# Reordering the second layer's experts in a four-layer cross-attention kernel: shared experts first, router picks between them

## The chip, the cores and the metric

The kernel runs on one core of a Trainium2 chip as a single program. The metric is the device time of that program in microseconds (us), as the median of several runs. The core has four engines that compute and that are ordered among each other only by semaphores: TensorE (PE, matrix products), VectorE (DVE, elementwise work and reductions), ScalarE (ACT, activation functions) and GpSimd (POOL, elementwise work). SyncE (SP) issues the transfers.

## The reference, cut to what matters

Four layers, each a cross-attention and a feed-forward, run over `x` (8 x 56 = 448 tokens of width 128). The change is in the feed-forward of layer 1, counted from 0. It is a mixture of 16 routed experts, of which each token takes the two with the highest logits, weighted by a sigmoid, and of a shared expert of width 256 that every token takes with weight one:

```
logits = jnp.einsum('btc,ec->bte', x, router_w)
top_vals, top_idx = jax.lax.top_k(logits, TOP_K)          # TOP_K = 2
gates = jax.nn.sigmoid(top_vals)
w_full = zeros((N, E)).at[arange(N)[:, None], sel].add(gw)
h = jax.nn.silu(gate) * up                                # all 16 experts, all tokens
out_all = jnp.einsum('neh,ehc->nec', h, down_w)
moe = jnp.einsum('ne,nec->nc', w_full, out_all)
shared = silu(x @ shared_gate_w.T) * (x @ shared_up_w.T) @ shared_down_w.T
return moe + shared
```

The result times `tanh(g_ffn[1])` is added to `x`. The order of the sum over experts doesn't matter but for rounding.

## The kernel before, in words

The kernel computes all 16 routed experts for all tokens, and cuts the shared expert into two of width 128. So there are 18 equal experts (`E1 = 18`), each with a weight per token: the tile `wts` holds 18 columns for each of 4 groups of 112 tokens. Columns 0 to 15 are the picks times the sigmoid of the logits, columns 16 and 17 are one. The experts' matrices lie in DRAM in the order of their use, three to a load (`load_experts1`, L581, G1 = 3), in two buffers.

For expert e these steps are taken, each released by a semaphore:

- PE, `gate_up1` (L1037): two products of 128x448 for gate and up, recorded as four matmuls (L1042), into two of four banks of PSUM.
- ACT, `silu1` (L1466): silu of the gate (L1468).
- DVE, `hidden1` (L2171): silu times up, into one of two tiles; recorded at L1740, as every two-operand operation of DVE is, since the helper `tt` issues it.
- PE, the second half of `expert1` (L1046): four products by the down matrix, eight matmuls (L1055), into bank 6 or 7. It waits for `hidden1(e)` and for `weigh(e - 2)`, which empties the bank.
- DVE, `weigh` (L2175): the product out of PSUM times the expert's weight, into one of two halves of `big` (L1740, 112x512).
- POOL, `add_expert` (L1669): adds that half to the accumulator `y2` (L1671). For the first expert it waits for `weigh(0)` alone.

On PE, `expert1(e)` first issues `gate_up1(e + 1)` and then the down product of e, so PE's stream is gate-up 0, gate-up 1, down 0, gate-up 2, down 1, gate-up 3, down 2, and so on. The order of each engine's work is written by hand; nothing is planned by a program. DVE takes its instructions strictly in the order of the text.

`pick(v, n, k, low)` (L2149) finds the k-th pick of each token: seven small operations, each waiting for the one before: a maximum (L2154), a comparison, a product with a constant row of ranks, a maximum (L2157), a comparison, and then either the masking of the pick (L2160, k = 0) or the sum of both picks (k = 1). Between the picks and the loop stand three pieces of DVE work: a product of two columns (128x1) and the scaling of `w_kT2` by it (L2199), which a later layer needs; the product of picks and sigmoid into `wts`; and the memset of the two shared columns (L2202). `Chain.link` issues an operation and waits for its end before the next; `Chain.step` issues it without the wait. The loop of the other experts begins at L2207.

ACT does silu 0, silu 1, the sigmoid of the logits (L1473) and then the other silus. Silu and sigmoid need different function tables, so an ACT_TABLE_LOAD stands ahead of each switch.

Of the kernel before, what the change touches and what calls it, by code (L numbers as in the profile page):

```python
# [11 lines left out]
ALU = mybir.AluOpType  # L12
# [3 lines left out]
D = 128  # L16
# [14 lines left out]
E1 = 18  # L31
# [84 lines left out]
G1 = 3  # L116
# [76 lines left out]
def build(nc, io, out):  # L193
    ctx = ExitStack()
    with ctx:
# [54 lines left out]
        def cs(name, rows=D):  # L250
            a, b = CST[name]
            return cst[0:rows, a:b]
# [11 lines left out]
        def carve(shape, dt=F32):  # L264
            n = int(np.prod(shape[1:]))
            words = n if dt == F32 else (n + 1) // 2
            a = arena[0:shape[0], at[0]:at[0] + words]
            at[0] += words
            assert at[0] <= ARENA, at[0]
            if dt != F32:  # L270
                a = a.bitcast(dt)
            if len(shape) == 2:
                return a
            names = "abcd"[:len(shape) - 1]
            return a.rearrange("p (" + " ".join(names) + ") -> p " + " ".join(names),
                               **dict(zip(names[1:], shape[2:])))
# [74 lines left out]
        sm16 = carve([TT, 8, NT, 16])  # L351
        wts = carve([TT, NT, E1])
# [1381 lines left out]
        def _(dve):  # L1734
            ch = Chain(dve, dve_s)
# [3 lines left out]
            def tt(out, a, b, op):  # L1739
                return dve.tensor_tensor(out, a, b, op)  # L1740

            def over(col, shape):

                return col.unsqueeze(2).broadcast_to(shape)
# [404 lines left out]
            def pick(v, n, k, low):  # L2149


                rank = cs("rank", TT)[:, 0:n].unsqueeze(1).broadcast_to([TT, NT, n])
                src = v[:, k]
                ch.link(dve.tensor_reduce(acol[:, 0, :], src, AX.X, ALU.max))  # L2154
                ch.link(tt(v[:, 2], src, over(acol[:, 0, :], [TT, NT, n]), ALU.is_equal))
                ch.link(tt(v[:, 2], v[:, 2], rank, ALU.mult))
                ch.link(dve.tensor_reduce(acol[:, 1, :], v[:, 2], AX.X, ALU.max))  # L2157
                ch.link(tt(v[:, 3 + k], v[:, 2], over(acol[:, 1, :], [TT, NT, n]), ALU.is_equal))
                if k == 0:
                    ch.link(dve.scalar_tensor_tensor(v[:, 1], v[:, 3], low, src, ALU.mult, ALU.add))  # L2160
                else:
                    ch.link(tt(v[:, 5], v[:, 3], v[:, 4], ALU.add))
# [8 lines left out]
            def hidden1(e, p):  # L2171
                dve.wait_ge(ex_act, e + 1)
                tt((xT2, xT3)[p], ps[0:D, 3 + 2 * p, 0:N], exs[p], ALU.mult).then_inc(ex_h, 1)

            def weigh(e, p, weight, first):  # L2175

                dve.wait_ge(ex_dn, first + e + 1)
                dve.wait_ge(ex_acc, first + e + 1)
                tt(big[:, :, D * p:D * p + D], ps[0:TT, 6 + p, :].rearrange("p (t n) -> p t n", t=NT),
                   weight.broadcast_to([TT, NT, D]), ALU.mult).then_inc(ex_w, 1)  # L2180

            def weigh_last(k, e, weight, first):
# [5 lines left out]
                residual(k, big[:, :, D:2 * D])  # L2188
                dve.nop().then_inc(ex_acc, 1)

            hidden1(0, 0)
            dve.wait_ge(to_act, 1)
            pick(sm16, 16, 0, NEG)
            hidden1(1, 1)
            pick(sm16, 16, 1, NEG)

            dve.wait_ge(ld_m, 5 * 16)
            ch.link(tt(qk_col[:, 0:1], qk_col[:, 0:1], qk_col[:, 1:2], ALU.mult))
            ch.step(dve.tensor_scalar(w_kT2, w_kT2, qk_col[:, 0:1], 8.0, ALU.mult, ALU.mult))  # L2199
            act_in.next()  # L2200
            ch.step(tt(wts[:, :, 0:16], sm16[:, 5], sm16[:, 6], ALU.mult))
            ch.link(dve.memset(wts[:, :, 16:E1], 1.0))  # L2202

            weigh(0, 0, wts[:, :, 0:1], 0)
            hidden1(2, 0)
            weigh(1, 1, wts[:, :, 1:2], 0)
            with dve.Fori(1, E1 // 2 - 1) as i:  # L2207
                for p in range(2):
                    e = 2 * i + p
# [278 lines left out]
```

## Time and profile before

| | us |
|---|---|
| median of 3 runs | 856.37 (855.80 to 856.83) |
| the profiled execution, whole | 857.73 |
| its span (first to last instruction) | 855.9 |
| the experts of layer 1, from the first gate-up matmul to the last down matmul | 330.8 to 375.5 |
| PE busy | 754.6 (88%) |
| DVE busy | 609.3 (71%) |
| ACT busy | 418.5 (49%) |
| POOL busy | 329.4 (38%) |

Times in the rows are microseconds from the span's start. The busy shares are means over many stages with different limits, so the stage of the change has to be read by itself. A row of a timeline gives the start, the duration, the engine, the line of the code, the operation, output and inputs with their shapes, and in brackets how long the engine had been idle and what released it. Consecutive instructions of one kind are merged into one row with a count. DVE is pipelined: an instruction that waits for nothing starts before the recorded end of the one ahead.

### The profile page before, as it was taken

To read this page: it belongs to the slowest core of one execution; us is meant where nothing else is said; L and a number is where in the kernel's file an instruction comes from. 1 tells how busy PE (TensorE), PEld (TensorE's weight loads), DVE (VectorE), ACT (ScalarE), POOL (GpSimd) and SP (SyncE) were. 2 spreads that over 40 slices of the span, in tenths; PEclk is the share of its full clock that TensorE was granted. 3 is DMA by queue.
4 is the path that set the end of the run, shared out by engine and by line. 5 is a ranking of instruction groups with operands and counts; after the bars stand their busy time and mean duration, and the time that the engine had idled before them with its cause. 6 is when DMAs were issued, how large, how long until landed. Compare 5 with 4: busy or idle time off the path is not lost.

```text
span 855.9 us, 15688 instructions
## 1 busy us (share of the span) xinstructions
PE 754.6 (88%) x5632; PEld 496.1 (58%) x5632; DVE 609.3 (71%) x1264; ACT 418.5 (49%) x682; POOL 329.4 (38%) x255
## 2 busy tenths in 40 slices
PE   4599999996777979987899999997898998988997
PEld 3577777786445576653455555563246665654675
DVE  4789999998886665566555666568788997515653
ACT  2476666673465624424444545411047776734331
POOL 0665555553523602550677777721160100000111
PEclk9799999997888958999999999998869999899999
DMA  7256766432425530205023332026834767000220
GB/s 202 81 196 215 245 207 201 160 121 83 60 84 180 160 99 8 85 30 161 1 75 89 118 92 75 0 34 100 115 97 101 121 145 148 3 2 25 92 93 23
DMA packets 50583, 88.35 MB, mean 103 GB/s; under 512 B 17375, under 2 KB 34975, under 8 KB 50167
## 3 DMA queue, kind: packets, MB, share of 16 engines
q1 hardware_dynamic: 50518, 87.49, 38.1%
q8 instruction: 41, 0.67, 0.3%
q14 instruction: 24, 0.19, 0.1%
HBM read 61.97 MB, written 25.51 MB: 102 GB/s over the span
## 4 chain that ended last, share of the span: by engine, by line
PE 46%; DVE 37%; ACT 5%; issue 5%; POOL 4%; DMA 2%; SPq 0%; DVEq 0%; POOLq 0%; ACTq 0%
DVE arena L2341 8%; PE ps L1109 8%; DVE arena L1740 8%; PE ps L1099 6%; DVE rn L1895 4%; PE ps L1277 3%; DVE arena L1944 3%; PE ps L1042 3%; PE ps L1214 3%; PE ps L1287 3%; DVE arena L1923 2%; PE ps L1203 2%; DVE arena L1903 2%; POOL arena L1694 2%; ACT arena L1538 2%
## 5 line engine op out<-in xcount | busy, mean ns | idle before, releaser
L2341 DVE TENSOR_REDUCE arena<-ps 112x1 f32<-112x500 f32 x192 | 114.9, 669 | 15.9 <-PE ps L1186 15.8
L1740 DVE TENSOR_TENSOR arena<-ps,arena 128x448 f32<-128x448 f32 (+7 forms) x138 | 83.4, 629 | 58.4 <-ACT arena L1562 19.7
L1694 POOL TENSOR_TENSOR arena<-arena 125x448 f32<-125x448 f32 x96 | 109.5, 1141 | 24.2 <-ACT arena L1507 21.2
L1109 PE MATMUL ps<-arena 125*128 125x448 f32 (+1 forms) x208 | 97.1, 548 | 1.4 <-ACT arena L1507 0.9
L1538 ACT ACTIVATE arena<-ps 125x896 f32<-125x896 f32 x96 | 87.0, 917 | 21.8 <-PE ps L1203 21.6
L1507 ACT ACTIVATE arena<-arena,kbias 125x448 f32<-125x448 f32 x96 | 63.7, 668 | 65.3 <-DVE arena L1740 46.3
L1740 DVE TENSOR_TENSOR arena<-ps,rn 125x448 f32<-125x448 f32 x96 | 59.3, 618 | 47.7 <-PE ps L1099 43.3
L1099 PE MATMUL ps<-arena 128*125 128x448 f16 (+3 forms) x312 | 77.9, 360 | 3.0 <-DVEq L1751 3.0
L1099 PEld LDWEIGHTS ps<-arena 128*125 128x125 f16 (+1 forms) x312 | 40.9, 135 | 57.2 <-issue 42.3
L801 PE MATMUL ps<-w_k2h,arena 128*125 128x512 f16 x288 | 67.9, 388 | 6.8 <-ACT arena L1343 5.2
L1671 POOL TENSOR_TENSOR arena<-arena 112x512 f32<-112x512 f32 x24 | 30.4, 1267 | 89.5 <-DVE arena L1740 89.4
L1343 ACT ACTIVATE arena<-ps 125x512 f32<-125x512 f32 x96 | 55.8, 596 | 14.2 <-PE ps L801 11.1
L1214 PE MATMUL ps<-arena 125*32 125x168 f32 x768 | 49.9, 331 | 11.5 <-ACT arena L1538 8.7
L1895 DVE TENSOR_REDUCE rn<-arena 125x8 f32<-125x512 f32 x96 | 58.2, 677 | 0.0
L1186 PE MATMUL ps<-arena 64*112 64x500 f16 x192 | 54.8, 443 | 2.9 <-DVE arena L2341 1.5
L801 PEld LDWEIGHTS ps<-w_k2h,arena 128*125 128x125 f16 x288 | 39.2, 139 | 30.4 <-ACT arena L1343 8.3
L1589 POOL TENSOR_TENSOR arena<-arena 112x4 f32<-112x4 f32 x9 | 9.3, 1028 | 121.5 <-DVE arena L1764 113.7
L824 PE MATMUL ps<-w_l,arena 128*125 128x256 f32 x192 | 44.7, 390 | 4.3 <-ACT arena L1370 4.3
L1712 POOL COPY arena<-arena 125x1152 f32<-125x1152 f32 x8 | 9.2, 1147 | 97.0 <-PE ps L1218 84.8
L1109 PEld LDWEIGHTS ps<-arena 125*128 125x128 f32 (+1 forms) x208 | 37.8, 189 | 13.9 <-issue 8.4
L728 PE MATMUL ps<-w_k2h 128*128 128x512 f16 x192 | 45.6, 393 | 0.0
L1605 POOL TENSOR_TENSOR arena<-arena 128x500 f16<-128x500 f32 x24 | 29.2, 1218 | 40.8 <-ACT arena L1330 40.8
(305 smaller groups left out, 1496.1 us busy)
## 6 DMA issues: line engine op xcount, KB each, us to landing
arena<-in_ctxT SPq DMA_DIRECT2D x8, 750.0 KB, 8.1
d_cln<-arena SPq DMA_DIRECT2D x8, 750.0 KB
d_clnT<-arena SPq DMA_DIRECT2D x8, 750.0 KB
d_k<-arena SPq DMA_DIRECT2D x24, 250.0 KB
d_v<-arena SPq DMA_DIRECT2D x24, 250.0 KB
arena<-d_clnT SPq DMA_DIRECT2D x8, 750.0 KB
arena<-in_ctx SPq DMA_DIRECT2D x8, 672.0 KB
arena<-d_cln SPq DMA_DIRECT2D x8, 672.0 KB
```

Of the source, the lines that this page charges most:

```text
L801: mm = pe.matmul(ps[0:KP, k, :], clnT[p][:, a, KP * j:KP * j + KP], w_k2h[:, w, :], start=(n == 0), stop=(n == 2))
L1099: mm = pe.matmul(ps[0:rows, (t + p) % 2, 0:N].rearrange("p (h q) -> p h q", h=H8), clnT_s[p][:, a, cols:cols + rows], qtT[:, q, :, bass.ds ...
L1109: pe.matmul(ps[0:D, 4 + 2 * p, 0:N], cln_s[p][0:rows, t, :], pexp[(t + p) % 2][0:rows], start=(t == 0), stop=(t == KT)).then_inc(l2_pv, 1)
L1186: pe.matmul(ps[0:TT, max_bank(bn, u), 0:500], q.rearrange("p o h q -> p (o h q)"), kst[bn % 3][64 * r:64 * r + 64, g, 500 * third:500 * th ...
L1214: pe.matmul(ps[32 * g:32 * g + 32, 6, 0:168], v3s[p][:, t, 32 * g:32 * g + 32], p3[t % 2][:, 3 * g:3 * g + 3, :].rearrange("p h q -> p (h ...
L1343: act.activation(sqk[:, j % SQ, :], ps[0:KP, k, :], ACT.Square).then_inc(a_free, 1)
L1507: act.activation(pexp[(t + p) % 2][0:rows], sscl[(t + p) % 2][0:rows], ACT.Exp, bias=bias)\
L1538: act.activation(p3[t % 2].rearrange("p (k h) q -> p k (h q)", k=2), ps[0:KP, 2 * (t % 2):2 * (t % 2) + 2, 0:8 * S], ACT.Exp).then_inc(l3_ ...
L1694: ins = pool.tensor_tensor(psum2[p][0:rows], psum2[p][0:rows], pexp[(t + p) % 2][0:rows], ALU.add)
L1740: return dve.tensor_tensor(out, a, b, op)
L1895: dve.tensor_reduce(rn[:, bass.ds(turn - 1, 1), j, :].rearrange("p o h -> p (o h)"), sqk[:, j % SQ, :].rearrange("p (h d) -> p h d", h=H8) ...
L2341: dve.tensor_reduce(mx3[bn % 2][:, u % 2, u % 8 // 2, u // 8:u // 8 + 1], ps[0:TT, max_bank_of(bn, u), 0:500], AX.X, ALU.max).then_inc(l3_ ...
```

## The change

The two shared experts become experts 0 and 1, and the sixteen routed ones 2 to 17. Their columns in `wts` move along, and so do the matrices in DRAM. As their weight is one and is set ahead of everything, `weigh(0)` no longer stands behind the picks: it is issued between the two picks, and `weigh(1)` behind `hidden1(2)`. The column product, the scaling of `w_kT2` and the product into `wts` now follow `weigh(1)`, and the last of them is a `link`. The memset of the weights of one stands ahead of `hidden1(0)`. PE, ACT, POOL and SP have the same instructions as before.

```diff
+            ch.link(dve.memset(wts[:, :, 0:2], 1.0))
             hidden1(0, 0)
             dve.wait_ge(to_act, 1)
             pick(sm16, 16, 0, NEG)
             hidden1(1, 1)
+            weigh(0, 0, wts[:, :, 0:1], 0)
             pick(sm16, 16, 1, NEG)
+            hidden1(2, 0)
+            weigh(1, 1, wts[:, :, 1:2], 0)

             dve.wait_ge(ld_m, 5 * 16)
             ch.link(tt(qk_col[:, 0:1], qk_col[:, 0:1], qk_col[:, 1:2], ALU.mult))
             ch.step(dve.tensor_scalar(w_kT2, w_kT2, qk_col[:, 0:1], 8.0, ALU.mult, ALU.mult))
             act_in.next()
-            ch.step(tt(wts[:, :, 0:16], sm16[:, 5], sm16[:, 6], ALU.mult))
-            ch.link(dve.memset(wts[:, :, 16:E1], 1.0))
-
-            weigh(0, 0, wts[:, :, 0:1], 0)
-            hidden1(2, 0)
-            weigh(1, 1, wts[:, :, 1:2], 0)
+            ch.link(tt(wts[:, :, 2:E1], sm16[:, 5], sm16[:, 6], ALU.mult))
+
             with dve.Fori(1, E1 // 2 - 1) as i:
...
-        "L1_ex": np.concatenate([experts1, np.stack(shared1)]).reshape(-1, G1, D, 3 * D).transpose(0, 2, 1, 3)
+        "L1_ex": np.concatenate([np.stack(shared1), experts1]).reshape(-1, G1, D, 3 * D).transpose(0, 2, 1, 3)
```

## Rows read from the trace of the kernel before

**Rows 1.** The chain that ended last, shares of the span by engine.

```profile
PE 46%; DVE 37%; ACT 5%; issue 5%; POOL 4%; DMA 2%; SPq 0%; DVEq 0%; POOLq 0%; ACTq 0%
```

**Rows 2.** Stretches: us, busy us of PE, PEld, DVE, ACT, POOL, clock, DMA share, GB/s.

```profile
336.30:340.00 3.70, 3.08 (x18) 1.99 (x17) 3.48 (x12) 2.84 (x4) 0.97 (x1) 1.00 0.01 2
344.80:347.18 2.38, 2.38 (x14) 1.62 (x13) 1.22 (x2) 1.83 (x3) 1.26 (x2) 1.00 0.00 0
384.00:388.00 4.00, 3.93 (x6) 1.50 (x6) 1.35 (x3) 0.68 (x2) 0.52 (x1) 0.57 0.32 99
```

**Rows 3.** The waits of 330 to 376 us: in total, times, longest.

```profile
PE ps L1055 <- DVE arena L1740: 1.1, 2, 0.6
```

**Rows 4.** PE's timeline, 333.5 to 342.4 us: gate-up 3, down 2, gate-up 4, down 3.

```profile
337.16 1.67 PE L1042 MATMUL ps<-arena,wex 128*128 128x448 f32 x4
339.44 1.13 PE L1055 MATMUL ps<-wex,arena 128*112 128x128 f32 x8 [0.62 <-DVE arena L1740]
340.41 1.67 PE L1042 MATMUL ps<-arena,wex 128*128 128x448 f32 x4
341.91 0.71 PE L1055 MATMUL ps<-wex,arena 128*112 128x128 f32 x5
```

**Rows 5.** DVE's timeline in the same stretch.

```profile
335.21 0.62 DVE L1740 TENSOR_TENSOR arena<-ps,arena 128x448 f32<-128x448 f32 x1
335.76 0.21 DVE L2154 TENSOR_REDUCE arena<-arena 112x4 f32<-112x64 f32 x1
336.00 0.23 DVE L1740 TENSOR_TENSOR arena<-arena 112x64 f32<-112x64 f32 x1
336.26 0.23 DVE L1740 TENSOR_TENSOR arena<-arena,cst 112x64 f32<-112x64 f32 x1
...
338.17 0.69 DVE L1740 TENSOR_TENSOR arena<-ps,arena 112x512 f32<-112x512 f32 x1
```

**Rows 6.** The chain that ended last, 337 to 339 us: start, duration, piece.

```profile
337.29 0.17 DVE arena L1740
...
337.49 0.18 DVE arena L2199
...
337.89 0.22 DVE arena L1740
...
338.77 0.63 DVE arena L1740
```

**Rows 7.** ACT's timeline there, the third silu last.

```profile
337.49 0.54 ACT L1468 ACTIVATE arena<-ps 128x448 f32<-128x448 f32 x1
```

**Rows 8.** POOL's timeline, 326 to 342 us.

```profile
339.03 3.96 POOL L1671 TENSOR_TENSOR arena<-arena 112x512 f32<-112x512 f32 x3 [11.36 <-DVE arena L1740]
```

**Rows 9.** POOL and DVE at 797 to 801 us; that DVE form's durations, ns min/median/max.

```profile
798.18 1.27 POOL L1671 TENSOR_TENSOR arena<-arena 112x512 f32<-112x512 f32 x1 [23.30 <-DVE arena L1740]
...
798.46 2.08 DVE L1740 TENSOR_TENSOR arena<-wex,arena 128x1024 f16<-128x1024 f32 x1
...
L1740 DVE TENSOR_TENSOR arena<-wex,arena x8: 1224/1226/2078, 778.3 to 832.7; 128x1024 f16<-128x1024 f32 x8
```

**Rows 10.** The same two engines at 26 us; L1909's durations, ns min/median/max.

```profile
26.01 1.27 POOL L1597 TENSOR_TENSOR wex<-wex,vec 112x512 f32<-112x512 f32 x1
...
26.18 1.13 DVE L1909 TENSOR_SCALAR arena<-arena 125x12 f32<-125x12 f32 x1
...
L1909 DVE TENSOR_SCALAR arena<-arena x8: 173/173/1131, 15.1 to 163.0; 125x12 f32<-125x12 f32 x8
```

**Rows 11.** The same two at 416 us, and L1694's mean (ns) over the kernel.

```profile
416.42 0.47 DVE L1843 TENSOR_SCALAR arena<-arena,wscale 128x512 f32<-128x512 f32 x1
...
416.63 1.27 POOL L1694 TENSOR_TENSOR arena<-arena 125x448 f32<-125x448 f32 x1
...
L1694 POOL TENSOR_TENSOR arena<-arena 125x448 f32<-125x448 f32 x96 | 109.5, 1141 | 24.2 <-ACT arena L1507 21.2
```

**Rows 12.** The landing of the transfers into `wex`.

```profile
DMA to landing us min/median/max: 3.4/3.7/10.8
```

## The prediction

> **What bounds the kernel now.** I read the chain that ended last first. Half of it is PE, most of the rest DVE, and transfers are 2% [rows 1], so a delay inside the chain goes through to the end. Then the stage itself. In the steady part of the expert loop, one expert takes 2.38 us and PE is busy in all 2.38, with DVE at 1.22 and POOL at 1.26 [rows 2]: the loop is bound by PE, and nothing on DVE matters there while its work fits into the 1.16 us left over. The waits then say that in the whole stage PE stood for DVE twice, with 0.6 us the longest [rows 3]. PE's timeline places it: gate-up 3 starts at 337.16 and down 2 at 339.44, where the next gate-up 4 (340.41) is followed by down 3 at 341.91, 1.50 us later [rows 4]. Without the wait down 2 would start at 337.16 + 1.50 = 338.66. So 339.44 - 338.66 = 0.78 us can be had, and about 0.1 more because a down product behind a wait takes 339.44 to 340.41, 0.97 us, instead of 2.38 - 1.50 = 0.88. The change can give no more than 0.87 us, 0.10% of the kernel. What down 2 waits for is `hidden1(2)`, at 338.77 [rows 6], the last of a row of DVE instructions: `hidden1(1)` at 335.21, the second pick from 335.76 [rows 5], the column product at 337.29, the scaling at 337.49, the weights at 337.89 and `weigh(0)` at 338.17 [rows 5, 6].
>
> **The change part by part, DVE alone.** The memset goes ahead of `hidden1(0)`, where DVE waits for ACT: nothing. `hidden1(1)` stays at 335.21, as do all of ACT's steps. `weigh(0)` follows after 0.55 us (335.21 to 335.76), at 335.76; down 0 ended long before. It takes 0.69, and the next instruction starts 0.60 behind it (338.17 to 338.77) [rows 5, 6]. So the second pick moves from 335.76 to 336.36 and its end, where the column product stood, from 337.29 to 337.89. `hidden1(2)` also needs silu 2, which ends at 337.49 + 0.54 = 338.03 [rows 7]; with 0.04 for the release it could start at 338.07. That is 0.70 before its 338.77. Were this all, down 2 would be at 338.74.
>
> **What is then late.** `weigh(0)` also releases POOL. Before, POOL was idle for 11.36 us and started the first add at 339.03 [rows 8], that is 0.17 behind the end of `weigh(0)` (338.17 + 0.69), when DVE's remaining work read one operand from PSUM. Now the add starts at 335.76 + 0.69 + 0.17 = 336.62, in the middle of the second pick, whose comparisons and products have two operands in SBUF. What that costs the rows show at other places. At 798.18 the same add (1.27 us) is running when DVE comes with a two-operand instruction from SBUF at 798.46: it takes 2.08 instead of 1.23, so it began in effect at 799.31, 0.14 before the add's end [rows 9]. A tiny scaling of 125x12 behind a POOL instruction takes 1.13 instead of 0.17, again from 0.14 before POOL's end [rows 10]. The Trainium skill, SBUF — State Buffer, section "Who interferes with whom", gives it as a lock: a DVE instruction with two SBUF inputs, or in a two-port mode, and a GpSimd instruction that reads SBUF exclude each other for the whole instruction, and the one issued second waits. By that rule, too, POOL's add stops the pick, and the change that frees DVE's order has an engine beside it that takes the time back; without it the sum would be C's, below.
>
> Collision 1, in the pick. Its first comparison moves from 336.00 to 336.60, the product from 336.26 to 336.86 [rows 5]. The comparison is 0.02 ahead of the add; the product then meets it, and starts at 336.62 + 1.27 - 0.14 = 337.75 or, with the add itself held a little by the comparison, up to 337.9: 0.9 to 1.05 late. If the comparison is the one held, 337.75 - 336.60 = 1.15 late. I take 1.0. `hidden1(2)` is then at 337.89 + 1.0 = 338.89, +0.12 against before, and down 2 at 339.56.
>
> Collision 2, in the moved block. `weigh(1)` starts 0.55 behind, at 339.44, ends at 340.13 and releases the second add at 340.30. The column product stands at 339.44 + 0.60 = 340.04 and the scaling 0.20 behind it at 340.24 [rows 6], just ahead of the add. A scaling from SBUF delays a POOL instruction that starts 0.21 behind it by 0.13 (1.27 against 1.14 [rows 11]), that is until 0.34 after its own start; so the add runs from 340.58 to 341.85. The weights product, due 0.40 behind the scaling [rows 6] at 340.64, is held until 341.85 - 0.14 = 341.71 and ends at 341.93. If the add is first and the scaling is held, this is 0.1 later. Behind it stands all of DVE's queue: the loop's start, `hidden1(3)`, `weigh(2)`. The product is now waited for ahead of the loop's header. No row shows that header bare: before, it lay hidden in the 0.60 us between the starts of `weigh(0)` and `hidden1(2)` [rows 5, 6]. Between nothing and 0.60 I take 0.2, as it is a few register instructions, each shorter than the shortest row. `hidden1(3)` is at 342.13, ends 0.62 later at 342.75, and down 3 is at 342.79, where before it was at 341.91: +0.88, and with the 0.09 of a down product behind a wait, +0.97. PE itself would have been there at 339.56 + 0.97 + 1.50 = 342.03, so PE stands 0.90 ahead of down 2 and 0.76 ahead of down 3.
>
> After that `hidden1(4)` needs silu 4 (gate-up 4 ended by 342.2, silu done by 342.8) and DVE, free by 343.3; down 4 is due at 345.2. DVE has caught up, and the loop runs at 2.38 again, 0.97 late. The order of the experts changes no product: same shapes, and the same loads of three. The third load, issued behind down 2 and landing in 3.7 us [rows 12], moves by 0.1 and is needed only at gate-up 6, two periods later than down 3. SP's queue holds nothing else there. The rest of the kernel follows unchanged.
>
> The sum: the profiled execution took 857.73 whole with a span of 855.9, and would take 858.7 with 856.9. The median before is 1.36 lower than that execution; on its scale the forecast is 856.37 + 0.97 = 857.3.
>
> **The rivals.** (B) Only the first collision happens, or the weights product slips in ahead of the waiting add. Then it ends at 340.86, `hidden1(3)` by 341.8, before PE needs it, and only the +0.12 stays: 856.5. For it: the two starts differ by hundredths. Against: POOL has been waiting by then, and DVE leaves a gap. (C) The two engines don't collide, because an add whose operands are short on DVE's side lets it through: down 2 at 338.74 is 0.70 early, the block ends at 340.2, `hidden1(3)` at 341.1, just ahead of down 3's 341.21, and the gain stays whole: 855.7. For it: no row shows an operation of the pick itself beside an add. Against: rows 9 and 10, where a form of 12 elements was held like the one of 1024. (D) Slower than can be mistaken: PE's clock. It is granted 1.00, its upper level of 2.4 GHz, in the stretches of the stage shown [rows 2]. Two waits of 0.90 and 0.76 us within 4 us make PE less busy than anywhere in the expert stage so far. If the clock falls to 1.2 GHz behind them as it does at 384 to 388, where 4 us are granted 0.57 [rows 2], a PE that is the bound loses 0.43 x 4 = 1.7 us: 857.3 + 1.7 = 859.0. It decides from the two waits together; against it, that the stretch with the wait of 0.62, 336.3 to 340, is granted 1.00 [rows 2].
>
> **How the numbers follow.** A change of 0.2%, 1.7 us, is about what a measurement here can tell from none. Forecast 0.53, B 0.14, C 0.20, D 0.10, anything else 0.03. The forecast's own range is 856.5 to 858.4: 0.2 less or 0.4 more for the header, 0.15 either way for the first collision, and 0.5 for the medians, which spread over 855.80 to 856.83. C with that spread sets the low end at 855.2, D the high end at 858.9. Faster by 0.2% (below 854.66) is only C with luck in the clock of later stages: 0.04. Slower (above 858.08): nearly all of D and a seventh of the forecast, 0.17. The same: 0.79.
>
> **What would show it.** Right: the first add of POOL starts near 336.6; one small operation of the second pick takes over 1 us instead of 0.23; the weights product takes over 1 us; PE shows two waits, ahead of down 2 and of down 3, of 0.7 to 1.0 us. Wrong: if the small operations keep their 0.23 beside the add (C), if PE's second wait is missing (B), or if the granted clock is below 1.00 between 340 and 376 (D). If the stage from the first gate-up to the last down product isn't about 1 us longer, the prediction's mechanism has failed, wherever the median lies.

## The result, and the profile after

The changed kernel took 868.22 us in the median of 4 runs (865.38 to 869.9), the kernel before 856.09 (4 runs, 855.4 to 856.83): a ratio of 1.0121, 95% interval 1.009 to 1.0152. Every ratio in this document leaves out runs more than 1.5% above the fastest of their kernel; none of these eight is such a run. The forecast was 857.3, the range 855.2 to 858.9. It was wrong by 11 us. The profiled execution after took 868.92 whole, with a span of 867.1 against 855.9.

The stage that the prediction worked out did what it said. DVE's timeline of the kernel after (start, duration, line, operation; "x2" joins two neighbours):

```profile
334.22 1.22 DVE L1740 TENSOR_TENSOR arena<-ps,arena 128x448 f32<-128x448 f32 x2
335.36 0.21 DVE L2154 TENSOR_REDUCE arena<-arena 112x4 f32<-112x64 f32 x1
335.60 0.23 DVE L1740 TENSOR_TENSOR arena<-arena 112x64 f32<-112x64 f32 x1
335.86 1.17 DVE L1740 TENSOR_TENSOR arena<-arena,cst 112x64 f32<-112x64 f32 x1
337.06 0.22 DVE L2157 TENSOR_REDUCE arena<-arena 112x4 f32<-112x64 f32 x1
...
337.84 1.22 DVE L1740 TENSOR_TENSOR arena<-ps,arena 128x448 f32<-128x448 f32 x2
338.98 0.15 DVE L1740 TENSOR_TENSOR arena<-arena 128x1 f32<-128x1 f32 x1
339.16 1.60 DVE L2203 TENSOR_SCALAR arena<-arena 128x512 f32<-128x512 f32 x1
340.68 0.21 DVE L1740 TENSOR_TENSOR arena<-arena 112x64 f32<-112x64 f32 x1
341.12 0.62 DVE L1740 TENSOR_TENSOR arena<-ps,arena 128x448 f32<-128x448 f32 x1 [0.23 <-DVE arena L1740]
```

POOL's timeline of the same kernel, and then PE's:

```profile
335.61 1.33 POOL L1671 TENSOR_TENSOR arena<-arena 112x512 f32<-112x512 f32 x1 [8.96 <-DVE arena L1740]
339.20 1.27 POOL L1671 TENSOR_TENSOR arena<-arena 112x512 f32<-112x512 f32 x1 [2.26 <-DVE arena L1740]
```

```profile
338.52 1.13 PE L1055 MATMUL ps<-wex,arena 128*112 128x128 f32 x8 [0.69 <-DVE arena L1740]
339.48 1.67 PE L1042 MATMUL ps<-arena,wex 128*128 128x448 f32 x4
341.80 1.13 PE L1055 MATMUL ps<-wex,arena 128*112 128x128 f32 x8 [0.65 <-DVE arena L1740]
```

All this is about a microsecond earlier than in the trace before, because this execution came to the stage earlier; count from `hidden1(1)`, at 335.21 before [rows 5] and at 334.22 now. Collision 1 is there: the add starts at 335.61, and the pick's product takes 1.17 where it took 0.23 [rows 5]. Collision 2 is there too, with the scaling as its victim: 1.60 beside the add of 339.20. PE's timeline has two waits where it had one [rows 4], 0.69 and 0.65; the other wait of rows 3, of 0.51, lies ahead of the last down product (at 374.39 before), far behind the change. Down 2 comes 4.30 behind `hidden1(1)` (before 4.23), down 3 comes 7.58 behind (before 6.70): +0.88.

Now the whole kernel in stretches, the view that the prediction did not take. The borders are the first gate-up of layer 1's experts, their last down product, the first product at L1099, the first at L1145, and the start and end of layer 3's attention. First before, then after (columns: from and to, us, busy us of PE, PEld, DVE, ACT, POOL with their counts, granted clock, DMA share, GB/s):

```profile
330.77:375.49 44.72, 43.59 (x219) 29.29 (x219) 24.91 (x52) 21.59 (x28) 20.77 (x17) 1.00 0.16 53
375.49:408.56 33.07, 23.71 (x81) 10.74 (x79) 22.14 (x42) 11.52 (x20) 4.85 (x3) 0.94 0.41 112
408.56:561.61 153.05, 151.45 (x537) 81.76 (x537) 90.26 (x143) 75.48 (x109) 116.92 (x104) 0.99 0.22 63
561.61:609.34 47.73, 39.92 (x225) 22.14 (x224) 35.44 (x100) 2.53 (x5) 7.50 (x9) 0.93 0.55 81
609.34:758.37 149.03, 134.52 (x2504) 85.38 (x2504) 115.87 (x202) 99.69 (x121) 24.30 (x23) 0.90 0.50 98
```

```profile
329.71:375.47 45.76, 43.91 (x219) 29.20 (x219) 26.85 (x52) 21.59 (x28) 20.85 (x17) 1.00 0.16 52
375.47:410.03 34.56, 25.20 (x82) 12.24 (x80) 22.13 (x42) 11.52 (x20) 4.85 (x3) 0.90 0.41 107
410.03:564.29 154.26, 152.83 (x537) 82.27 (x537) 91.56 (x143) 75.50 (x109) 116.62 (x104) 0.98 0.21 63
564.29:611.93 47.64, 39.94 (x226) 21.99 (x225) 35.44 (x100) 2.54 (x5) 7.50 (x9) 0.93 0.55 86
611.93:769.06 157.13, 143.03 (x2504) 89.40 (x2504) 116.28 (x202) 100.59 (x121) 24.30 (x23) 0.84 0.44 92
```

Read the first row of each, and then the last. The stage is 45.76 - 44.72 = 1.04 longer, the forecast's +0.97. The code of every later stretch is the same in both kernels, POOL works as long as before, DVE too but for 1.30 us in the third row, and yet these stretches are 1.49, 1.21, -0.09 and 8.10 longer. In the stretches that grew, PE is busy for longer with as many instructions, and its granted clock is lower: 0.94 to 0.90, 0.99 to 0.98, 0.90 to 0.84. Outside these rows the start is 1.06 shorter and the tail 0.54 longer; all together that is the 11.2 between the spans.

Layer 3's attention runs in batches. In both kernels PE waits at L1214 once in each, and in five of them the wait is 0.89 us. Two of these waits on PE's timeline, before and then after:

```profile
646.80 0.49 PE L1214 MATMUL ps<-arena 125*32 125x168 f32 x8 [0.89 <-ACT arena L1538]
647.11 0.28 PE L1218 MATMUL ps<-arena 125*16 125x56 f32 x8
```

```profile
649.35 0.67 PE L1214 MATMUL ps<-arena 125*32 125x168 f32 x8 [0.89 <-ACT arena L1538]
649.77 0.43 PE L1218 MATMUL ps<-arena 125*16 125x56 f32 x8
```

The wait is the same, and what follows is not: right behind it the same eight matmuls take 0.67 instead of 0.49, as PE has fallen from its 2.4 GHz to 1.2 GHz. The stretches between such waits, before and then after:

```profile
646.80:662.62 15.82, 14.67 (x313) 10.02 (x313) 14.41 (x26) 12.12 (x16) 1.59 (x2) 1.00 0.60 124
662.62:678.45 15.83, 14.67 (x314) 10.02 (x314) 14.42 (x26) 12.13 (x16) 1.60 (x2) 1.00 0.71 124
```

```profile
649.35:666.59 17.24, 16.09 (x313) 10.67 (x313) 14.50 (x26) 12.28 (x16) 1.59 (x2) 0.90 0.55 113
666.59:683.81 17.22, 16.06 (x313) 10.69 (x314) 14.51 (x26) 12.29 (x16) 1.60 (x2) 0.90 0.58 115
```

A batch of 15.82 us at full clock becomes one of 17.24 with a part at half clock, PE 1.42 us longer busy, and the period longer by as much. DVE, busy for 14.4 of the 15.82, did not make up for it. The page shows it as a longer wait of DVE's reductions for PE, 22.7 us in all where it was 15.9:

```profile
L2341 DVE TENSOR_REDUCE arena<-ps 112x1 f32<-112x500 f32 x192 | 115.3, 668 | 22.7 <-PE ps L1186 22.7
```

So the open question was why a stage that is 1 us longer changes the clock in a stretch that starts 236 us after it. Two theories stood at the start, content and arrival; the third came when the kernel before turned out to spread. **Content**: the changed order itself, or the collisions, do something that lasts. **Arrival**: only when the later stretches begin decides, whatever delayed them. **Constant**: the change costs 12 us in every execution, against which stood that the time of one kernel may vary from execution to execution.

### The profile page after: what moved, and what is told of

Its sections match the earlier page's. It is cut to its first block, busy times and chain, and to the rows that moved or that the text cites. A ratio compares the mean times of both kernels' runs of the same rounds, so it can differ in the third digit from the quotient of the medians.

```text
span 867.1 us, 15689 instructions
## 1 busy us (share of the span) xinstructions
PE 765.8 (88%) x5632; PEld 502.0 (58%) x5632; DVE 614.2 (71%) x1264; ACT 419.6 (48%) x682; POOL 329.4 (38%) x255
## 4 chain that ended last, share of the span: by engine, by line
PE 46%; DVE 37%; issue 5%; ACT 5%; POOL 5%; DMA 2%; SPq 0%; DVEq 0%; POOLq 0%; ACTq 0%
PE ps L1109 8%; DVE arena L1740 8%; DVE arena L2341 7%; PE ps L1099 6%; DVE rn L1895 4%; PE ps L1214 3%; PE ps L1277 3%; DVE arena L1944 3%; PE ps L1287 2%; PE ps L1042 2%; PE ps L1203 2%; DVE arena L1923 2%; DVE arena L1903 2%; POOL arena L1694 2%; PE ps L1186 1%
## 5 line engine op out<-in xcount | busy, mean ns | idle before, releaser
L2341 DVE TENSOR_REDUCE arena<-ps 112x1 f32<-112x500 f32 x192 | 115.3, 668 | 22.7 <-PE ps L1186 22.7
L1694 POOL TENSOR_TENSOR arena<-arena 125x448 f32<-125x448 f32 x96 | 109.2, 1137 | 26.2 <-ACT arena L1507 23.3
L1099 PE MATMUL ps<-arena 128*125 128x448 f16 (+3 forms) x312 | 78.1, 360 | 3.0 <-DVEq L1751 3.0
L1099 PEld LDWEIGHTS ps<-arena 128*125 128x125 f16 (+1 forms) x312 | 40.9, 135 | 57.8 <-issue 42.4
L801 PE MATMUL ps<-w_k2h,arena 128*125 128x512 f16 x288 | 66.0, 380 | 7.2 <-ACT arena L1343 5.6
L1214 PE MATMUL ps<-arena 125*32 125x168 f32 x768 | 53.2, 350 | 11.2 <-ACT arena L1538 7.9
L1186 PE MATMUL ps<-arena 64*112 64x500 f16 x192 | 56.6, 462 | 2.8 <-DVE arena L2341 1.3
L1895 DVE TENSOR_REDUCE rn<-arena 125x8 f32<-125x512 f32 x96 | 58.2, 674 | 0.0
L1203 PE MATMUL ps<-arena 64*125 64x112 f16 x768 | 46.6, 247 | 0.0
```

Source lines behind the costliest of these rows:

```text
L801: mm = pe.matmul(ps[0:KP, k, :], clnT[p][:, a, KP * j:KP * j + KP], w_k2h[:, w, :], start=(n == 0), stop=(n == 2))
L1099: mm = pe.matmul(ps[0:rows, (t + p) % 2, 0:N].rearrange("p (h q) -> p h q", h=H8), clnT_s[p][:, a, cols:cols + rows], qtT[:, q, :, bass.ds ...
L1186: pe.matmul(ps[0:TT, max_bank(bn, u), 0:500], q.rearrange("p o h q -> p (o h q)"), kst[bn % 3][64 * r:64 * r + 64, g, 500 * third:500 * th ...
L1203: mm = pe.matmul(ps[0:KP, 2 * (t % 2) + r, 112 * g:112 * g + 112], kst[b % 3][rows, g, KP * t:KP * t + KP], qst3[rows, b:b + 1, g, 2 * r:2 ...
L1214: pe.matmul(ps[32 * g:32 * g + 32, 6, 0:168], v3s[p][:, t, 32 * g:32 * g + 32], p3[t % 2][:, 3 * g:3 * g + 3, :].rearrange("p h q -> p (h ...
L1694: ins = pool.tensor_tensor(psum2[p][0:rows], psum2[p][0:rows], pexp[(t + p) % 2][0:rows], ALU.add)
```

## The experiments

Edits are against the kernel before unless it says "after". Each result is the median over all executions with the range and their count, beside the kernel before on the same chip at the same time. Since here the spread is itself the effect, I give the difference of the means over all runs as well, with its 95% interval. The lengths of stretches are worked out from the records of each trace, as in the two tables above: E the expert stage, P the preparation behind it, A2 and A3 the attention of layers 2 and 3, counted from 0. Behind a length stands, in brackets, how much of it was granted the lower clock:

```
                  E             P             A2            A3           span
before       44.72 (0)     33.07 (3.7)   153.05 (3.2)  149.03 (30.7)  855.9
after        45.76 (0)     34.56 (6.8)   154.26 (6.8)  157.13 (51.2)  867.1
e5  = after  45.77 (0)     34.57 (6.8)   154.28 (6.8)  153.15 (44.4)  861.7
e15 = after  45.76 (0)     31.38 (0)     153.03 (3.4)  149.71 (30.7)  855.9
e1           45.73 (0)     34.58 (6.8)   154.26 (6.8)  156.14 (47.8)  866.0
e9           45.22 (0)     35.28 (10.2)  152.68 (3.4)  152.71 (44.4)  860.4
e10          48.43 (3.4)   34.57 (6.8)   154.27 (6.8)  157.27 (51.2)  867.5
e2           44.35 (0)     33.08 (3.5)   153.04 (3.3)  149.70 (30.7)  856.9
e3           44.19 (0)     33.63 (7.2)   153.04 (3.1)  149.28 (30.7)  855.3
e4           44.80 (0)     33.09 (3.8)   153.05 (3.1)  149.47 (30.7)  854.2
e11          44.09 (0)     33.61 (7.0)   153.04 (3.2)  149.19 (30.7)  854.5
e16 = e11    44.09 (0)     33.62 (7.0)   153.04 (3.2)  149.32 (30.7)  855.5
e6           44.71 (0)     33.07 (3.7)   153.04 (3.2)  149.13 (30.7)  855.8
e12          44.71 (0)     33.60 (7.6)   155.55 (9.5)  149.90 (30.7)  859.8
e13          44.72 (0)     33.08 (3.6)   153.04 (3.2)  154.73 (47.8)  859.5
e14          44.71 (0)     35.29 (10.2)  152.92 (3.4)  154.81 (47.8)  859.8
```

### A bare delay in the kernel before

```diff
 weigh(0, ...)
+for _ in range(4):
+    ch.link(dve.tensor_reduce(acol[:, 1, :], sm16[:, 2], AX.X, ALU.max))
 hidden1(2, 0)
```

> The kernel before with four small reductions (112x64 to 112x4, each waited for, some 0.245 us each) put ahead of hidden1(2): nothing of the change, only its delay of 1.0 us at the same place. Theory clock (the stage itself is 1.0 us longer, the other 11 us are PE's clock at its lower level in later stages, set by how late the work of those stages arrives): 867 to 869 us, with the stage 1.0 longer and the same stretches at half clock as in the changed kernel. Theory content (the rest comes from something else that the change brings, such as the new order of weights or POOL's earlier adds): 857.1.

It took 865.33 (855.77 to 869.65, n 10) against 860.46 (852.32 to 867.53, n 31): ratio 1.0014 [0.9965, 1.0063], difference of the means +3.8 ± 3.4. The median lies 2 below the 867 to 869 that were expected. The trace is the clear part. With the order, the adds and the scaling of before, and 1.01 us of delay, the trace has the stretches of after nearly to the hundredth (34.58, 154.26, 156.14). Its last stretch:

```profile
612.04:768.18 156.14, 141.50 (x2503) 88.48 (x2504) 116.33 (x202) 100.40 (x121) 24.33 (x23) 0.85 0.44 92
```

Content falls: neither the new order nor a collision is needed. The median of before beside this run, 860.46 and not 856, was the first sign that 4 executions were too few.

The same with 2 and with 8 reductions, to see whether the loss grows with the delay or has a threshold:

> The kernel before with two reductions (0.5 us in all) ahead of hidden1(2), half of the delay of the run with four. The four profiles of kernels with a stage 1.0 us longer all show half-clock stretches near 393, 400 and 410 to 417 where the others show one at 384 and one at 408, and need 3.7 us more from the down products to 415 us. Theory threshold (which stretches are granted turns over at some arrival between 0.15 and 1.0 us late): the profile shows one pattern or the other whole, so +0.5 or about +3.2 to 3.7 at 415 us, nothing between. Theory proportional: about +1.9.

> The same with eight reductions, 2.0 us. Theory threshold: the stretches follow the arrival in bands, so twice the delay need not cost more than the 1.0 us did: between +2 and +5 at 415 us. Theory proportional: about +7.4.

e9 took 861.52 (858.06 to 867.67, n 10) against 858.12 (853.9 to 868.63, n 35), 1.0034 [1.0005, 1.0064], means +2.6 ± 2.2; e10 took 863.52 (860.13 to 869.24, n 10), 1.0044 [1.0012, 1.0075], +4.9 ± 2.2. A stage that is 0.50 longer has 3.7 more in A3; one that is 3.71 longer has 8.2 in A3, as after has. The loss is not in proportion to the delay. Neither theory's numbers came, though: from the first gate-up to the end of A2, e9 is 2.3 longer and e10 6.4, where threshold wanted 0.5 or 3.2 to 3.7 and 2 to 5, and proportional 1.9 and 7.4; e9 shows a third pattern of falls, with 10.2 us in P. e10 also shows rival D's mechanism, at a larger wait than the change makes. PE's timeline of e10:

```profile
337.29 1.13 PE L1055 MATMUL ps<-wex,arena 128*112 128x128 f32 x8 [2.65 <-DVE arena L1740]
338.25 2.87 PE L1042 MATMUL ps<-arena,wex 128*128 128x448 f32 x4
340.92 1.57 PE L1055 MATMUL ps<-wex,arena 128*112 128x128 f32 x8
```

Behind a wait of 2.65 us the gate-up takes 2.87 instead of 1.67: 3.4 us at half clock. This is why 2 us of delay made the stage 3.71 longer.

### The two collisions

Hold POOL's adds back (on after), or scale `w_kT2` ahead of `hidden1(0, 0)` (on before, on after), or both (on after):

```diff
 # e2, e11, e16: POOL's loop of the adds
+if e == 0:
+    pool.wait_ge(ex_h, 5)
 pool.wait_ge(ex_acc, e + 2)
 # e3, e4, e11, e16: the three lines moved up
+dve.wait_ge(ld_m, 5 * 16)
+ch.link(tt(qk_col[:, 0:1], qk_col[:, 0:1], qk_col[:, 1:2], ALU.mult))
+ch.step(dve.tensor_scalar(w_kT2, w_kT2, qk_col[:, 0:1], 8.0, ...))
 hidden1(0, 0)
```

> The changed kernel, but POOL's first add also waits for hidden1(3), so that it runs beside no operation of the pick and of the moved block. If the collisions with POOL are what makes the stage 1.0 us longer, the stage gets 0.7 us shorter than before the change and no small DVE operation takes over 0.3 us. Theory clock: the whole then follows from where -0.7 us puts the later stages, which nobody can say from the rows: anything from 850 to 866, with the difference to 855.4 in the stretches at half clock. Theory content: 866.

> The kernel before with the column product and the scaling of w_kT2 moved ahead of hidden1(0), where DVE waits for ACT. down 2 waits 0.6 us less, so the stage is 0.6 us shorter; no add is near. Theory clock: 855.5 if the later stages keep their stretches at half clock, several us more or less if not. Theory content: 855.5 in any case.

> The changed kernel with the same move: the first collision (pick against add) stays, the second has nothing left but the weights product, which comes 0.2 us before the second add. The stage is 0.1 to 0.2 us longer than before the change. Theory clock: at 0.15 us the later stages lie almost as in the kernel before: 856 to 857. Theory content: 867.

> The changed kernel with both causes of its longer stage taken away: the scaling of w_kT2 ahead of hidden1(0), and POOL's first add behind hidden1(3). The stage is 0.7 to 0.8 us shorter than before the change, no DVE operation of the pick is stretched. Mean over executions 0 to 3 us below the kernel before, if the later stages keep their usual stretches; if any move of the stage were bad, above it.

> The version with the scaling early and the first add late once more. Mean 0.5 to 2 us below the kernel before; rival: no difference, or above.

The expert stage answers each edit, against 44.72 before and 45.76 after. The adds held back take 1.41 off after's stage (44.35); 0.7 less than before was expected, and it is 0.37. The scaling moved ahead takes 0.96 off after's (44.80) and 0.53 off before's (44.19). Both together give 44.09, 0.63 less than before and 1.67 less than after. But e3 has 0.53 of this without any of the reordering, so the new order adds only 0.10 to it. DVE's timeline of e11, where nothing is held and each small operation is back at 0.23:

```profile
334.98 0.23 DVE L1742 TENSOR_TENSOR arena<-arena 112x64 f32<-112x64 f32 x1
335.24 0.23 DVE L1742 TENSOR_TENSOR arena<-arena,cst 112x64 f32<-112x64 f32 x1
335.50 0.22 DVE L2159 TENSOR_REDUCE arena<-arena 112x4 f32<-112x64 f32 x1
```

Of PE's waits for DVE only the one of 0.5 us ahead of the last down product is listed; of the one ahead of down 2, 0.62 before, 0.15 is left (down 2 is 1.65 behind its gate-up, where the loop has 1.50):

```profile
PE ps L1055 <- DVE arena L1742: 0.5, 1, 0.5
```

The version that shows what the collisions cost is e2, as it differs from after in nothing but the held add. Counted from the first gate-up, its down 2 and down 3 come at 8.04 and 10.51, where before has 8.67 and 11.14 and after 8.81 and 12.10. So the mechanism is shown: the two engines' collisions turned a gain of 0.63 at these steps (the forecast for DVE alone was 0.70) into a loss. Holding the add has a price of its own, which leaves e2 with 0.37 at the stage's end. DVE then stands 1.62 us for POOL ahead of `weigh(2)`, and down 4 and the gate-up behind it come 0.17 and 0.27 later than in e11, where DVE has the scaling behind it already:

```profile
342.76 3.38 DVE L1742 TENSOR_TENSOR arena<-ps,arena 112x512 f32<-112x512 f32 x5 [1.62 <-POOL arena L1671]
```

The whole kernels do not follow. In medians, against 860.46 for e2 to e4, 858.12 (e11) and 857.75 (e16): e2 858.99 (854.3 to 866.38, n 10), ratio 0.9993 [0.995, 1.0036]; e3 858.53 (856.77 to 866.84, n 10), 0.9985 [0.9949, 1.0021]; e4 857.93 (853.16 to 866.73, n 10), 1.0005 [0.9963, 1.0047]; e11 857.01 (854.93 to 865.81, n 12), 0.9987 [0.9958, 1.0016]; e16, the same kernel, 859.49 (856.12 to 867.15, n 12), 1.0033 [1.0002, 1.0064]. By means e11 is 1.3 below before and e16 1.5 above; pooled, 24 executions against the 67 of before beside them, they are 0.1 ± 1.6 us from it. The version that was to beat both kernels beats after and equals before; a gain of 0.63 is below what this spread lets one see.

### The same kernel again: constant or not

> The changed kernel itself, beside the kernel before on one chip, with more executions of both. The kernel before has meanwhile been seen from 852 to 867 us, so four executions of each may have caught two ends. Theory mixture (a real effect of 1.0 us, the rest is which half-clock stretches an execution gets): the median lies 1 to 5 us above the median before, with the two ranges overlapping. Theory constant (the change costs 12 us in every execution): the median lies 10 to 13 us above and the ranges hardly overlap.

> The changed kernel once more. Mean 3 to 5 us above the kernel before of the same chip; the first comparison's 12 us was four draws from each end. Rival: near 12.

After unchanged, twice. e5: 863.64 (853.85 to 870.48, n 12) against 857.31 (852.09 to 869.05, n 28), 1.0037 [0.9997, 1.0076], means +4.1 ± 3.4. e15: 866.09 (853.49 to 871.05, n 12), 1.0034 [0.9989, 1.008], +5.75 ± 3.5. The profile of e15 has the same stage, 45.76, with the same two held operations, and then none of the loss. The two rows of e15 that answer to P and A3:

```profile
376.01:407.39 31.38, 22.02 (x82) 10.22 (x80) 22.14 (x42) 11.52 (x20) 4.85 (x3) 1.00 0.44 118
608.32:758.03 149.71, 134.53 (x2504) 85.46 (x2504) 115.79 (x202) 99.74 (x121) 24.33 (x23) 0.90 0.47 97
```

Its batches take 15.82 at a clock of 1.00, as those of before do. So the same code loses 8 us in A3 in one execution (the profile after), 4.1 in another (e5) and 0.7 in a third. Constant falls. Over all runs behind the first comparison the kernel before has 126 executions between 852.09 and 869.05 (mean 859.2, median 858.2), and after has 24 between 853.49 and 871.05 (mean 863.7, median 865.1). 14% of the first lie above 864, and 14 of the 24. Against the 60 executions of before beside them (mean 858.8), the means differ by 5.0 ± 2.4 us, 0.6%. That is the best estimate of what the change costs; the first comparison, with four executions of before that all fell at 855.4 to 856.83, put it at 12.

### A delay far from the experts

The arrival theory has a sharper test: leave the experts of layer 1 alone and come a little later to layer 3. e6 adds one small reduction on DVE ahead of `maxima(b)`, inside the attention. e13 and e14 add one and two ahead of the scaling of layer 3's queries, which everything behind waits for:

```diff
+ch.link(dve.tensor_reduce(acol[:, 1, :], lnst, AX.X, ALU.max))   # e14: twice
 ch.link(dve.tensor_scalar(xT2, ps[0:D, 1, 0:N], float(D) ** -0.5, ...
```

> The kernel before with one reduction (112x24 to 112x4, some 0.2 us with its wait) put on DVE ahead of the first maximum of layer 3's attention; the experts of layer 1 are untouched. Theory arrival (whether PE's clock falls once in each batch of layer 3's attention depends on tenths of a microsecond in the arrival of that stage): the profiled execution shows stretches at half clock between 645 and 760 us as the changed kernel's did, and takes 864 to 867. Theory amount (it takes the whole microsecond, or something in the experts stage): the profile of the stage stays as before, 856.6.

> The kernel before with one reduction (112x24 to 112x4, some 0.2 us with its wait) on DVE's chain of products that make layer 3's queries, near 600 us; the experts of layer 1 untouched. Theory arrival: all profiles in which the work of this stage comes 0.15 to 0.3 us later show half-clock stretches once in a batch and 152 to 157 us for layer 3's attention, the others none and 149; so here the attention takes 152 to 157. Rival (the stretches need the whole late state from 390 us on): 149.1.

> The same with two reductions, 0.4 us. Theory arrival: the bad band begins between 0 and 0.2 us and was seen up to 1.4 us later in the run with a delay of 0.5 us, so 152 to 157 for the attention here too. Rival: 149.1.

e6 took 859.29 (855.11 to 862.51, n 12), 1.0018 [0.9993, 1.0043]. A3 stayed at 149.13: the delay was hidden behind a wait for PE, so it tested nothing and is inconclusive. e13 took 861.61 (853.58 to 865.91, n 10) against 857.75 (852.38 to 866.19, n 32), 1.0031 [0.9995, 1.0067], means +2.4 ± 2.4. e14 took 861.76 (859.6 to 866.1, n 7), 1.0056 [1.0021, 1.0091], +4.2 ± 2.0. In e13's trace everything up to layer 3 is as before (44.72, 33.08, 153.04), the stretch with the added reduction is 0.23 longer, and then:

```profile
607.78:762.51 154.73, 141.97 (x2504) 88.75 (x2504) 116.25 (x202) 100.65 (x121) 24.33 (x23) 0.85 0.44 93
645.19:661.95 16.76, 16.03 (x313) 10.59 (x313) 14.07 (x25) 11.86 (x15) 1.59 (x2) 0.90 0.53 116
```

Against 609.34:758.37, an instruction of 0.2 us is followed by 5.70 more in the attention, with the clock at 0.85 instead of 0.90 and PE busy 7.45 longer. This is one profile each, of kernels whose executions spread, and the means of e13 hardly leave zero. e14 shows why a single profile can mislead: its P is 35.29 with 10.2 us at half clock, though its edit lies 230 us behind P, so that execution was in a late state by itself.

What supports arrival more is in the traces together: they record when the granted clock changes, and arrival has to be counted from there, not from the span's start. Take PE's last rise to the upper clock ahead of A3 (589.21 in before, the end of the fall near 582). A3's first product comes 19.92 to 20.19 us behind it in the nine traces whose batches have no fall (before 20.14, e15 19.98, the latest e3 and e4 with 20.19), and 20.28 to 20.43 in six of the seven whose batches have (after 20.43, e1 20.38, e13 20.32, e14 20.28); the seventh, e9, whose fall near 585 lasted 3.4 us and not 6.8 as in the others, has 22.38. From the span's start the two groups are mixed: e13 falls with 607.77, e12 does not with 611.86. P is ordered alike, by the end of the expert stage behind the last rise ahead of the stage (326.38 in before): 48.47 to 49.18 with 3.5 to 7.6 us at half clock, 49.63 and 49.88 with 10.2 (e9, e14), 50.06 to 50.21 with 6.8 (e1, e5, after), and 50.50 with none (e15); e10 has 53.51, with a fall inside the stage. Equal code draws its place here: the first gate-up comes 4.29, 4.44 and 4.74 behind that rise in e5, after and e15. So arrival holds: each execution draws its place against the clock's changes, the edit adds its delay to it, and 0.2 us can decide. That is a reading of sixteen traces, made behind the runs; the one edit that moves A3's arrival alone is e13, from before's 20.14 to 20.32.

### Attempts to keep the clock up

Fill PE's waits: at the first step of each batch the max product is repeated three times into its own bank (e7 on after, e8 on before), meant for the wait of 0.89 us. Or fill most of PE's wait at 381.1 to 382.9 us with more of the kernel's own keep-busy products (e12):

```diff
 # e7, e8
+for _ in range(3 if t == 0 and n else 0):
+    pe.matmul(...)                        # the same product as the next
 pe.matmul(ps[0:TT, bank, 0:500], ...)
 # e12
-keep_clock(26, 3)
+keep_clock(33, 3)
```

> The changed kernel with three extra matmuls of 64x112 by 500 in each batch of layer 3's attention but the last, repeating the one behind them in the text, ahead of the place where PE waits 0.89 us for ACT once in a batch. Theory: this wait is what the clock falls behind (at 649.35 the wait ends, at 649.5 the clock falls). Then the wait shrinks to 0.1 to 0.3, no half-clock stretch stands between 645 and 725, and the median is 7 to 9 us lower than the changed kernel's. Rival: the stretches come from elsewhere in the batch, or DVE's maxima wait for the extra matmuls: same or slower.

> The kernel before with the same three extra matmuls for each batch. Theory: its own executions above 860 us are those with the half-clock stretches in layer 3's attention, so the median falls from about 860 to 855, the range narrows to some 6 us, and the difference between this and the changed kernel with the same matmuls is 1.0 us plus what the stretches at 384 to 417 us give (up to 4). Rival: no effect on the range.

> The kernel before with 33 instead of 26 dummy matmuls behind the experts, which fill 1.5 of the 1.8 us in which PE waits at 381.1 to 382.9 for the layer norm. Theory: the clock falls at 384.4 behind that wait, and the 3.4 us at half clock there cost 1.7 us; with the gap filled there is no fall at 384 and the span is 1 to 2 us shorter, unless a fall moves to the gaps at 391 to 409 behind it. Rival: the wait has no part in the fall, same time.

e7 took 867.86 (861.91 to 869.14, n 6), ratio 1.0113 [1.0078, 1.0148], means +8.0 ± 2.7; e8 took 861.98 (856.19 to 869.3, n 11), 1.0057 [1.0024, 1.009], +3.8 ± 2.9. The products missed the wait. It is 0.89 in both kernels still; only the first one, of 1.58, shrank to 0.33. Two of e8's waits, with no fall near:

```profile
646.39 0.49 PE L1219 MATMUL ps<-arena 125*32 125x168 f32 x8 [0.89 <-ACT arena L1543]
662.79 0.49 PE L1219 MATMUL ps<-arena 125*32 125x168 f32 x8 [0.89 <-ACT arena L1543]
```

The batch between them takes 16.40 where before has 15.82, so the products lie on the path and cost 0.58 us in each at full clock. In e7 batches with a part at half clock stayed. Whether the fall comes from the 0.89 us wait is therefore not tested by either run. e12 took 861.64 (858.42 to 864.59, n 12), 1.0027 [1.0004, 1.0051], +2.5 ± 1.5: the wait shrank from 1.83 to 0.31 and the half clock at 384 went, and more of it came later, 7.6 us in P and 9.5 in A2 where there were 3.7 and 3.2. The rows of e12:

```profile
374.77:408.37 33.60, 25.76 (x89) 12.11 (x87) 22.13 (x42) 11.51 (x20) 4.84 (x3) 0.89 0.44 110
408.37:563.92 155.55, 154.12 (x537) 82.85 (x538) 91.12 (x143) 75.50 (x109) 116.74 (x104) 0.97 0.21 62
```

All three expectations of a gain were missed, and e8's range did not narrow.

## Why the prediction was wrong

- **DVE alone (-0.70): right.** In e2, where no add is near, down 2 comes 3.53 behind `hidden1(1)` (339.02 and 335.49 in its timelines), 0.70 less than the 4.23 before, and down 3 is 0.70 earlier as well. A small term was missed: from the first gate-up to `hidden1(1)` it is 4.51 in after, e2 and e15 and 4.44 before. Those 0.07, with the +0.88 of down 3 and the 0.09 of a down product behind a wait, are the 1.04. The memset alone does not make them: e4, e11 and e16 have it and show 4.44 to 4.45; what does is open. That e2 keeps only 0.37 at the stage's end is the cost of holding the add, above.
- **Collision 1: right, in place and price.** The add began 0.17 behind the end of `weigh(0)`, as forecast, the comparison kept its 0.23, the product took 1.17 against 0.23: 0.94 late (forecast 1.0). Down 2 stands +0.07 against `hidden1(1)` (forecast +0.12). The Trainium skill, SBUF — State Buffer, section "Who interferes with whom", says that the one that comes second is blocked for the whole instruction, not slowed, and that a reduction never is; the trace agrees. The 64-element product takes 1.17. The pick's own reduction, at 337.06, came behind the add's end and shows nothing, but in the trace of before 87 reductions at L1895 (125x512) lie beside a POOL instruction and take 0.67 to 0.68 us, as the nine others do.
- **Collision 2: right in sum, wrong in its victim.** The scaling was to be just ahead of the add and the weights product held. In the trace the scaling's record starts 0.04 before the add's and it is the one held, 1.60 against 0.49; the product then took its 0.21. The prediction had this as its alternative, "0.1 later", and the loop's header cost 0.23 (forecast 0.2). Down 3: +0.88, as forecast, with some luck: down 2 came 0.05 less late than forecast, and the way from there to down 3 was 0.05 longer. The stage: +1.04 against +0.97.
- **Rivals B and C: out**, by PE's second wait and by the held operations. One sum of C was off: its own steps from 338.07 end at 340.04, not 340.2; nothing hangs on it. **Rival D: out in its place.** The stage is granted 1.00 behind two waits of 0.69 and 0.65; it took one of 2.65 to bring the clock down there (e10).
- **"The rest of the kernel follows unchanged": this is the step that failed.** It was true of the instructions and false of their durations. The later stretches grew by 1.49, 1.21 and 8.10 us with the clock. The warning stood in the rows: before's own 384 to 388 us is granted 0.57 [rows 2], so this kernel's clock falls behind waits that it has anyway, and I asked only whether the change makes a new wait, not whether it shifts the old ones. The traces of e1 and e13 show that shifting them by 1.0 or 0.2 us is enough, and the sixteen traces, that what decides is where the stage starts behind the clock's last rise.
- **"0.2%, about what a measurement here can tell": too small.** It rested on three executions within 1.03 us. Over 126 the same kernel spreads over 17 us (2%). The range ought to have been several times as wide upward, as before itself lies above 864 in one of seven executions.

What stays open is how a given execution will come out. The executions differ from each other already before the experts of layer 1 (the first stretch is 326.6 to 331.0 us in the sixteen traces, with 51 to 61 us at half clock), so each execution reaches the later waits at another moment, and none of this can be known ahead. Nor does a run here change the length of the 0.89 us wait. The Trainium skill, TensorE: Matmul & The Clock Gate, section "Part 1: The HAM clock gate (the "warmup" mystery)", says that the chip watches the engine's activity independently of the kernel's start, so that one kernel's half-clock part varies by run. No run here looks at that counter itself; that e5, e15 and after differ with equal code agrees with it. The same section puts the penalty of the ramp, the half-clock part when the engine starts to work, at under 1% of a typical kernel. No run here measures that ramp alone; with the later falls one kernel spreads over 2% here. How much of the first 12 us was luck is open too, beyond that 24 executions against 60 say 5.0 ± 2.4.

## What to carry to other kernels

An edit that frees one engine's order also frees the engine behind it, and if the two hold each other up, as DVE and POOL do here, the freed one can take back more than was gained: find what the moved step releases, and hold that back or move the long operation beside it away, as e11 does. In a kernel whose clock already falls behind some of its waits, a shift of 0.2 to 1.0 us could re-draw those falls far away, in stretches that the edit does not touch. So give the range the size of that draw, measure tens of executions before believing a difference of 1%, and when you compare traces count a stage's start from the clock's last rise.

## What the runs showed of the hardware

- The time of a single execution of one kernel on one core goes from 852.1 to 869.05 us, in step with how long its PE was at half clock: over the 126 executions of before the correlation is 0.89, some 0.30 us of time per us at half clock (worked out from each run's mean granted clock).
- PE's identical wait of 0.89 us is followed by half clock in some executions and not in others, and where it is, a batch in which DVE is busy for 14.4 of 15.8 us still becomes 1.42 us longer. Which it is goes with the start of that attention behind the clock's last rise: 19.92 to 20.19 us without falls, 20.28 and more with them, in sixteen traces.
- Between a DVE and a POOL instruction that start within hundredths, the order of the recorded starts does not tell which is held: at 339.16 it was the earlier one.
- A loop's header behind a wait costs DVE 0.23 us that nothing hides (340.89 to 341.12 in after, and 0.23 in e2, e4 and e11 too).
